# A two-layer graph network on one core: TensorE signals from its queue behind a drain, VectorE reads weights and column numbers from PSUM

## What is computed

```
h = relu(layernorm(x))
x = x + relu(segment_sum((h @ W)[edge sources] * dinv[src] * dinv[dst]) + b)     # first edge layer, GCN with its own loops
h = relu(layernorm(x))
# second edge layer, attention of 8 heads of 16; src and dst are given in sorted order
q = h[src] @ Wq.T + bq ; k, v = h[dst] @ Wk.T + bk, h[dst] @ Wv.T + bv
e   = exp(clip(sum(q * k per head) / 4, -10, 10))
out = segment_sum(e / (segment_sum(e, src)[src] + 1e-8) * v, src)
x = x + layernorm(out + h) * gamma + beta
```

## Time and profile before

| | us |
|---|---|
| median of 3 runs | 2849.39 |
| lowest, highest | 2832.88, 2861.96 |
| the profiled execution | 2854.68 |
| its span, first to last instruction | 2852.4 |
| busy in it: PE, DVE, ACT, POOL | 1823.0, 1832.7, 1265.2, 1532.9 |
| mean granted TensorE clock | 0.798 |

### The profile page before, as it was taken

The page is one execution under the profiler, slowest core; times in us unless marked ns, Lnnn a source line. Parts: engine busy times, 40 slices in busy tenths (PEclk is TensorE's granted clock), DMA queues, the critical chain, the costliest instruction groups (busy, mean ns, idle before and its releaser), DMA issues. The chain is left out here.

```text
span 2852.4 us, 43311 instructions
## 1 busy us (share of the span) xinstructions
PE 1823.0 (64%) x10081; PEld 1438.6 (50%) x10082; DVE 1832.7 (64%) x4977; ACT 1265.2 (44%) x3328; POOL 1532.9 (54%) x1595
## 2 busy tenths in 40 slices
PE   5324346766677666766786776766777667677672
PEld 4324334444434444443464666665666566666561
DVE  9858785655555654655574666566666666666666
ACT  8524345756556564655563323233333223233333
POOL 0266666666556565565625555545555555555555
PEclk7766667877878788877898878788888888888886
DMA  3211111111111111111107444445444444445453
GB/s 108 60 45 44 44 40 42 42 44 41 42 37 45 39 42 41 38 42 40 41 27 218 123 127 125 122 118 130 124 125 125 121 123 133 121 123 137 121 124 56
DMA packets 227714, 238.31 MB, mean 84 GB/s; under 512 B 32381, under 2 KB 189565, under 8 KB 227557
## 3 DMA queue, kind: packets, MB, share of 16 engines
q0 software_dynamic: 59984, 143.85, 18.7%
q1 hardware_dynamic: 138133, 79.45, 11.0%
q10 hardware_dynamic: 29568, 14.68, 2.1%
HBM read 219.25 MB, written 18.62 MB: 83 GB/s over the span
## 5 line engine op out<-in xcount | busy, mean ns | idle before, releaser
L303 POOL DMA_INDIRECT rows<-y_tab,idx x832 | 795.6, 956 | 566.9 <-issue 304.8
L1382 POOL DMA_INDIRECT x<-kv_tab,kv_idx x648 | 658.6, 1016 | 592.9 <-DVE msg L1434 384.2
L1605 PE MATMUL ps_kv<-kv_s,hot_low 128*128 x1314 | 405.9, 455 | 147.2 <-DVE hot_low L1406 79.9
L782 ACT ACTIVATE sort_v<-sort_t,staged,minus 128x128 f16<-128x128 f16 x914 | 360.6, 480 | 305.6 <-remote 241.8
L874 PE MATMUL ps_sort<-sort_hi,sort_v 128*128 128x496 f16 x1662 | 416.1, 400 | 123.5 <-issue 122.2
L621 DVE TENSOR_SCALAR sort_v<-iota_h,staged 128x128 f16<-128x128 f16 x748 | 243.9, 326 | 315.1 <-remote 266.2
L1592 PE MATMUL ps_m<-msg,x 128*128 128x136 f32 x1728 | 289.7, 319 | 206.9 <-DVE msg L1434 152.6
L832 PE MATMUL ps_sum<-rows,hot 128*128 128x128 f32 x1664 | 275.6, 321 | 216.6 <-issue 102.2
L1605 PEld LDWEIGHTS ps_kv<-kv_s,hot_low 128*128 128x128 f32 x1314 | 282.9, 230 | 199.4 <-issue 161.1
L832 PEld LDWEIGHTS ps_sum<-rows,hot 128*128 128x128 f32 x1664 | 255.3, 233 | 237.6 <-issue 149.5
L1592 PEld LDWEIGHTS ps_m<-msg,x 128*128 128x128 f32 x1728 | 258.2, 222 | 225.6 <-issue 218.1
(11 more groups left out here) (290 smaller groups left out, 2129.6 us busy)
## 6 DMA issues: line engine op xcount, KB each, us to landing
weights<-tile_tab SPq DMA_DIRECT2D x110, 256.0 KB
x<-tile_tab SPq DMA_DIRECT2D x109, 256.0 KB
weights<-tile_tab ACTq DMA_DIRECT2D x56, 256.0 KB
rows<-y_tab,idx POOLq DMA_INDIRECT x832
x<-kv_tab,kv_idx POOLq DMA_INDIRECT x648
...
```

The costliest lines, as they stand in the source:

```text
L303: pool.indirect_dma_start(out=rows[:, k * SPAN + n, :], out_offset=None, in_=y_tab, in_offset=bass.IndirectOffsetOnAxis(ap=idx[:, k, n:n + ...
L782: last = nc.scalar.activation(to[:, k % 2, m, :], sort_t[:, k % 2, m, :], ACT.Relu, bias=staged[:, v, c:c + 1], scale=minus[:, v, c:c + 1])
L1382: pool.indirect_dma_start(out=rows[:, u, k, :], out_offset=None, in_=kv_tab, in_offset=bass.IndirectOffsetOnAxis(ap=idx[:, u, k:k + 1], ax ...
L1605: last = nc.tensor.matmul(ps_kv[:, k % 2, :], hot_low[:, w, k * P:(k + 1) * P], kv_s[:, ds(low + w, 1), :], start=w == 0, stop=w == WINDOW ...
```

## The change

Three parts.

1. First layer: the increments of `sum_done`, `more_done` and `moved` are taken off the matmuls. Behind each group stands `pe.drain(fusable=False)`, an instruction of TensorE's queue that ends when the engine has finished, and it carries the increment.
2. Second layer: one drain for each quad, behind sums, fill and expand. It raises `q_ready`, and two queue instructions behind it raise `sum_done` and `fill_done`.
3. Second layer, operands: ScalarE's Exp is done twice, into a PSUM tile `ps_w`, which VectorE's `values` reads, and into `msg`, which TensorE's `sums` reads after a new wait for `w_kept`. The numbers 1 to 128 lie in unused columns of the `ps_m` banks, where `one_hot` reads them. For the bank of `ps_w`, `ps_off` moves to SBUF as `src_off`.

```diff
@@ -829,9 +829,9 @@
                 def sums(ps, k, hots, done):
 
                     for n in range(SPAN):
-                        last = nc.tensor.matmul(ps[:, 0:D], hots[:, n, :], rows[:, k * SPAN + n, :],
-                                                start=n == 0, stop=n == SPAN - 1)
-                    last.then_inc(done, 1)
+                        nc.tensor.matmul(ps[:, 0:D], hots[:, n, :], rows[:, k * SPAN + n, :],
+                                         start=n == 0, stop=n == SPAN - 1)
+                    pe.drain(fusable=False).then_inc(done, 1)
 
                 def edges(i, beside, last=False):
 
@@ -871,9 +871,9 @@
                             pe.wait_ge(v1_ready[k], n + 2)
                             for m in range(sorts[k]):
                                 for values, ps in ((sort_v1, ps_sort[part][0]), (sort_v2, ps_sort[part][1])):
-                                    last = nc.tensor.matmul(ps[:, 0:w], values[:, k % 2, m, :], sort_hi[:, k % 2, m, 0:w],
-                                                            start=False, stop=False)
-                            last.then_inc(moved[k], 1)
+                                    nc.tensor.matmul(ps[:, 0:w], values[:, k % 2, m, :], sort_hi[:, k % 2, m, 0:w],
+                                                     start=False, stop=False)
+                            pe.drain(fusable=False).then_inc(moved[k], 1)
                         edges(n + RANK_BODIES, move, sorts is LAST_SORTS)
 
                     with pe.Fori(begin, begin + PART_BODIES[part] - part) as n:
@@ -1317,7 +1317,8 @@
             att = sb4("att", [P, 2, QUAD * HEADS])
             attc = sb4("attc", [P, 2, QUAD * HEADS])
             msg = sb4("msg", [P, QUADS, QUAD, MSG])
-            ps_off = ps4("ps_off", [P, QUAD * P])
+            off = sb4("src_off", [P, QUAD * P])
+            ps_w = ps4("ps_weights", [P, QUAD, HEADS])
             ps_kv = ps4("ps_kv", [P, 2, 2 * D])
             ps_q = [ps4(f"ps_q{k}", [P, QUAD, D]) for k in range(2)]
             ps_m = [[ps4(f"ps_m{k}{g}", [P, 2, 256]) for g in range(2)] for k in range(2)]
@@ -1330,6 +1331,7 @@
             prod_done, clip_done, w_ready, msg_ready, sum_done, acc_done = (
                 per_quad("prod_done"), per_quad("clip_done"), per_quad("w_ready"), per_quad("msg_ready"),
                 per_quad("sum_done"), per_quad("acc_done"))
+            w_kept = sem("w_kept")
             att_done = sem("att_done")
             tile_added = sem("tile_added")
             low_in, hot_low_ready, fill_done, filled = (
@@ -1393,9 +1395,10 @@
 
                 def one_hot(i, u):
 
-                    nc.vector.tensor_tensor(hot[:, u, :, :],
-                                            iota[:, 1:P + 1].unsqueeze(1).to_broadcast([P, QUAD, P]),
-                                            src_t[:, columns(i, u)].unsqueeze(2).to_broadcast([P, QUAD, P]),
+                    in_halves = lambda t: t.rearrange("p k (g c) -> p k g c", g=2)
+                    nc.vector.tensor_tensor(in_halves(hot[:, u, :, :]),
+                                            ps_m[u % 2][0][:, :, MSG:MSG + P // 2].unsqueeze(1).to_broadcast([P, QUAD, 2, P // 2]),
+                                            src_t[:, columns(i, u)].unsqueeze(2).unsqueeze(3).to_broadcast([P, QUAD, 2, P // 2]),
                                             ALU.is_equal).then_inc(hot_ready[u], 1)
 
                 def hots_of_low(i):
@@ -1434,7 +1437,7 @@
                     nc.vector.tensor_tensor(
                         msg[:, u, :, 0:D].rearrange("p t (h c) -> p t h c", c=HD),
                         rows[:, u, :, D:2 * D].rearrange("p t (h c) -> p t h c", c=HD),
-                        msg[:, u, :, D:MSG].unsqueeze(3).to_broadcast([P, QUAD, HEADS, HD]),
+                        ps_w[:, :, :].unsqueeze(3).to_broadcast([P, QUAD, HEADS, HD]),
                         ALU.mult).then_inc(msg_ready[u], 1)
 
                 def add_sums(i, u, k, b):
@@ -1480,6 +1483,9 @@
 
                 nc.vector.tensor_scalar(minus_lane[:, :], lane[:, :], -1.0, -1.0, ALU.mult, ALU.add).then_inc(lane_set, 1)
                 then(nc.vector.tensor_scalar(lanes[:, :], iota[:, 0:WINDOWS], float(P), lane[:, :], ALU.mult, ALU.add))
+                for n in range(2):
+                    last = nc.vector.tensor_copy(ps_m[n][0][:, :, MSG:MSG + P // 2], iota[:, 1:P + 1].rearrange("p (g c) -> p g c", g=2))
+                then(last)
                 v.wait_ge(low_in, 16)
                 for w in range(WINDOWS):
                     last = nc.vector.tensor_scalar(hot_low[:, w, :], from_low, lanes[:, w:w + 1], None, ALU.is_equal)
@@ -1526,7 +1532,7 @@
                         act.wait_ge(hotT_ready[u - 1], i + 1)
                     elif not (isinstance(i, int) and i == 0):
                         act.wait_ge(hotT_ready[QUADS - 1], i)
-                    nc.scalar.activation(ps_off[:, :], from_src[u % 2], ACT.Abs, bias=minus_lane[:, :]).then_inc(off_made, 1)
+                    nc.scalar.activation(off[:, :], from_src[u % 2], ACT.Abs, bias=minus_lane[:, :]).then_inc(off_made, 1)
 
                 def hot_of_src(i, u):
 
@@ -1535,7 +1541,7 @@
                         act.wait_ge(q_ready[u - 2], i + 1)
                     elif not (isinstance(i, int) and i == 0):
                         act.wait_ge(q_ready[u + 2], i)
-                    nc.scalar.activation(hotT[:, u % 2, :, :], ps_off[:, :].rearrange("p (k d) -> p k d", k=QUAD), ACT.Relu,
+                    nc.scalar.activation(hotT[:, u % 2, :, :], off[:, :].rearrange("p (k d) -> p k d", k=QUAD), ACT.Relu,
                                          bias=1.0, scale=-1.0).then_inc(hotT_ready[u], 1)
 
                 load_low(act, 0)
@@ -1560,8 +1566,9 @@
                         act.wait_ge(clip_done[u], i + 1)
 
                         act.wait_ge(acc_done[u], i + 1)
-                        nc.scalar.activation(msg[:, u, :, D:MSG], attc[:, u % 2, :].rearrange("p (t h) -> p t h", h=HEADS),
-                                             ACT.Exp, scale=0.25).then_inc(w_ready[u], 1)
+                        clipped = attc[:, u % 2, :].rearrange("p (t h) -> p t h", h=HEADS)
+                        nc.scalar.activation(ps_w[:, :, :], clipped, ACT.Exp, scale=0.25).then_inc(w_ready[u], 1)
+                        nc.scalar.activation(msg[:, u, :, D:MSG], clipped, ACT.Exp, scale=0.25).then_inc(w_kept, 1)
                         distance(i if u < 1 else i + 1, (u + 3) % QUADS)
                         if u < QUADS - 1:
                             set_idx(i + 1, u)
@@ -1578,20 +1585,19 @@
 
                     pe.wait_ge(prod_done[(u - 2) % QUADS], i + 2 if u >= 2 else i + 1)
                     for k in range(QUAD):
-                        last = nc.tensor.matmul(ps_q[u % 2][:, k, :], hotT[:, u % 2, k, :], q[:, ds(buckets[k], 1), :],
-                                                start=True, stop=True)
-                    last.then_inc(q_ready[u], 1)
+                        nc.tensor.matmul(ps_q[u % 2][:, k, :], hotT[:, u % 2, k, :], q[:, ds(buckets[k], 1), :],
+                                         start=True, stop=True)
 
                 def sums(i, u):
 
                     pe.wait_ge(hot_ready[u], i + 1)
                     pe.wait_ge(msg_ready[u], i + 2)
+                    pe.wait_ge(w_kept, i * QUADS + u + 1)
 
                     pe.wait_ge(acc_done[(u - 2) % QUADS], i + 2 if u >= 2 else i + 1)
                     for k in range(QUAD):
-                        last = nc.tensor.matmul(ps_m[u % 2][k // 2][:, k % 2, 0:MSG], hot[:, u, k, :], msg[:, u, k, :],
-                                                start=True, stop=True)
-                    last.then_inc(sum_done[u], 1)
+                        nc.tensor.matmul(ps_m[u % 2][k // 2][:, k % 2, 0:MSG], hot[:, u, k, :], msg[:, u, k, :],
+                                         start=True, stop=True)
 
                 def fill(i, k, low):
 
@@ -1602,21 +1608,25 @@
                     if k % 2 == 0 and not (isinstance(i, int) and i == 0 and k == 0):
                         pe.wait_ge(filled, i * 2 + k // 2)
                     for w in range(WINDOWS):
-                        last = nc.tensor.matmul(ps_kv[:, k % 2, :], hot_low[:, w, k * P:(k + 1) * P], kv_s[:, ds(low + w, 1), :],
-                                                start=w == 0, stop=w == WINDOWS - 1)
-                    last.then_inc(fill_done, 1)
+                        nc.tensor.matmul(ps_kv[:, k % 2, :], hot_low[:, w, k * P:(k + 1) * P], kv_s[:, ds(low + w, 1), :],
+                                         start=w == 0, stop=w == WINDOWS - 1)
 
                 begun = of_pass(mybir.EngineType.PE, 0, slice(2 * QUAD, GROUP + QUAD))
-                expand(0, 0, begun[0:QUAD])
-                expand(0, 1, begun[QUAD:2 * QUAD])
+                for u in range(2):
+                    expand(0, u, begun[u * QUAD:(u + 1) * QUAD])
+                    pe.drain(fusable=False).then_inc(q_ready[u], 1)
```

(4 more changed lines are left out.)

## The result

| | before | after |
|---|---|---|
| median, us | 2855.68 (4 runs) | 3205.51 (4 runs) |
| lowest, highest | 2832.88, 2870.78 | 3196.6, 3233.63 |
| profiled execution, its span | 2854.68, 2852.4 | 3197.04, 3195.3 |
| mean granted clock | 0.798 | 0.799 |

The changed kernel is slower: 1.128 times the time before, 95% interval 1.122 to 1.134. The clock is the same, so it has no part in it.

A forecast was written before the change was run, and what follows sets the result against it. It took both layers to be bound by engines waiting for one another, on late matmul signals. From 2854.7 us it took 127 (second layer) and 108 (first), giving 2620, less 5 for the timed median: 2615 us, range 2470 to 2870.

The forecast's parts named there:

- Signals that ride on matmuls are late ... I read the gathers as what delays them: Both layers: TensorE's signals come late, by 2.8 us on the mean, delayed by GpSimd's gathers; a reading called not proven.
- The 2.8 us: Second layer: mean of the 63 waits of VectorE at L1416, taken as the signals' mean lateness.
- What a drain costs ... I take the first: Both layers: beside gathers a drain by itself costs 0.05 us, the lower bound, not the present lateness of 2.8 us.
- the array has done the work and only the message is missing: TensorE, second layer: matmuls starting at full pace behind a late signal were taken to show the work is finished.
- the slower rival: Drains end as late as the signals and block TensorE's queue: 452 bubbles add 125 us, 2980 us or more; chance 0.18.
- The bubble is 0.3 to 0.4 us: TensorE, both layers: gap behind each of 452 drains, 181 us if all exposed, nothing if hidden in idle time.
- GpSimd is next, at 40: First layer: GpSimd's 32 gathers bound a sorting body at 40 us; 45.4 was forecast instead of 50.8, gaining 108 us.
- the floors of 40 and 18.3 us: Lowest times for a first-layer sorting body and a second-layer pass; the forecast took the middle, 45.4 and 20.65 us.
- I leave as they are: First layer: the five bodies before the sorting bodies were forecast to keep their time.
- Operands "at nothing": Second layer: weights and column numbers from PSUM and the second Exp were forecast to change the time by nothing.
- Signals gathered behind one drain: Second layer: `sum_done` and `fill_done` come 2.3 us later, with `q_ready`; at most 65 us, hidden while TensorE sets the pace.
- my new pace: Second layer: a pass falls from 23.0 to 20.65 us, TensorE's 3.5 us a quad setting the pace; gain 127 us.

The follow-up runs named there:

- e5: Kernel before with both layers' gathers replaced by plain transfers of the same size from fixed rows, issued from SyncE's queue: 2369 us.
- e7: Kernel before with both layers' gathers replaced by plain transfers of the same size from fixed rows, still issued from GpSimd's queue: 2055 us.
- e12: Kernel before with two small GpSimd instructions, each waited for, behind each gather as a real pause: 3607 us.
- e16: Kernel before with one small GpSimd instruction, waited for, behind each second gather: 2716 us, ratio 0.956.
- e4: Kernel before with all increments left on the matmuls and bare drains, which nobody waits for, behind the same groups in both layers: 3144 us, ratio 1.098.
- e8: Kernel before with 48 tiny VectorE instructions at the head of each sorting body, the last one waited for: 2901 us.
- e6: Changed kernel with the gathers replaced by plain transfers of the same size from fixed rows, issued from SyncE's queue: 2599 us.
- e18: Changed kernel with one small GpSimd instruction, waited for, behind each second gather: 2749 us.
- e17: Kernel before with one small GpSimd instruction, waited for, behind each fourth gather: 2591 us, ratio 0.913.
- e3: Changed kernel with all drains undone and increments back on the matmuls, so only the operands part is left: 2910 us, ratio 1.021.
- e14: Kernel before with only the column numbers 1 to 128 read from the ps_m banks: 2935 us, ratio 1.014.
- e15: Kernel before with only the weights part (second Exp, TensorE's wait for it, source distances in SBUF): 2933 us, ratio 1.012.
- e2: Kernel before with only the second layer's drain and increments for each quad, no operand moved: 2961 us.

## Why the prediction was wrong

- **"Signals that ride on matmuls are late ... I read the gathers as what delays them": right, as far as recorded runs can tell.** e5, e7, e12 and e16 take the gathers, their form or their density away, and the lateness goes with each. The 2.8 us are the mean of VectorE's waits, not of the lateness, which was 3 us beside dense gathers: near it by chance.
- **"What a drain costs ... I take the first": the step that failed.** I had two bounds, 0.05 us and the present lateness, 2.8 us, and took the lower on a row without gathers. That row could not tell: with no gather under way the signals are not late either. The drains are late by 1.8 to 5.3 us on the mean beside dense gathers, so the upper bound was the one to take, and while a drain waits TensorE's queue is blocked, which by e4 alone costs 290 of the 350 us.
- **Its second reason, "the array has done the work and only the message is missing", read more into the earlier trace rows than stands there.** A timeline records the starts of matmuls and models the ends. Starts at full pace show that TensorE can begin; they don't show that anything has been completed. The other sign lay in the earlier trace rows, three matmuls in 1.40 us with 0.90 us before them: starts that slow down while work is outstanding, which e8 shows on VectorE too. I had it among the reasons for the slower rival and gave that 0.18.
- **"The bubble is 0.3 to 0.4 us": mis-sized.** By the medians of e6 TensorE starts again 0.44 us behind a drain of the first layer and 0.75 in the second, 0.16 us of overlap are lost too, and the bodies of e6 lose 0.73 us a drain, the lower clock in it.
- **The slower rival: right in its mechanism, a third in its size.** It gave 2980 us, 125 of the 350 us lost, bubbles only, "and more where the next quad's sums could have run". By e4 the blocked queue, its bubbles among it, costs 290 us. How much of that is bubbles, longer than I had them, and how much the queue held for the time of the lateness, isn't separated. That it is not the bubbles alone, e18 suggests: the same drains with nothing late cost 33 us there, though GpSimd, near its own pace, may hide part of them.
- **"GpSimd is next, at 40", the floors of 40 and 18.3 us: neither refuted nor shown.** e17's 46.8 and 19.4 us stand above them. Its body is near GpSimd's own time with the pauses, 24 x 1.25 + 8 x 1.81 = 44.5 us. The 18.3 us held the clock at 0.84, and e17's passes were granted 0.94, by the same formula 1 / (0.88 / 15.6 + 0.12 / 28.8) = 16.5 us. That its 2591 us is near the 2615 that I forecast is luck: another change got there, with late signals as frequent as before and a higher clock.
- **The ranking bodies, "I leave as they are": wrong.** They lost 31 us, and the stretch between the last body and the first pass 17.
- **Operands "at nothing": wrong by 2%** (e3, e14, e15), cause open. The gathers became shorter, as said (1016 to 947 ns), off the path, as said.
- **"Signals gathered behind one drain": named, but hidden only in my new pace.** They are one candidate for the 0.8 us a pass between e2 and e4; the queue instructions behind the drain, 0.34 us a quad, which I had at nothing, are the other.

Two rules of the Trainium skill bear on this. The page "TensorE: Matmul & The Clock Gate", section "The cost: per-tile semaphore tail", calls an increment on the last matmul sound, and its formula gives a tail of some 56 ns for one tile and one increment, an estimate. Where nothing crowds it the trace does not contradict that (0.01 us behind the end in e5, e7 and e12, but that end is modelled, so the tail itself can't be read); beside dense gathers it does (3 us on the mean). The page "PSUM — Partial Sum Buffer", section "Engine vs sequencer instructions", has a drain wait until the engine is fully idle. The traces agree in so far as the drain ends late where signals do and 0.02 us behind the matmuls where they don't. What in the engine is still open in the late time they don't show.
